# An int4 transformer layer: the down weights are dequantised inside the gate and up stage and pass through DRAM, with three direct pairs in place of five

## The reference

```python
w = stack([W_q >> 4 & 15, W_q & 15], axis=-1)          # per group of 64: (w - zero) * scale
g = x2 @ Wg.T ; u = x2 @ Wu.T                          # x2 = layernorm(x1), Wg and Wu: [2752, 1024]
h = silu(g) * u
out = x1 + layernorm(h @ Wd.T)                         # Wd: [1024, 2752]
```

## Time and profile before

| what | value |
|---|---|
| median of three runs | 2843.83 us |
| the profiled execution's own time | 2843.78 us |
| its span, first to last instruction | 2842.0 us |
| PE, DVE, ACT, POOL busy | 93%, 55%, 34%, 43% of the span |
| mean granted TensorE clock | 0.97 |
| time of a step in the 40 slices | 71 us |

### The profile page before, as it was taken

The page is one execution under the profiler, slowest core; times in us unless marked ns, Lnnn a source line. Parts: engine busy times, 40 slices in busy tenths (PEclk is TensorE's granted clock), DMA queues, the critical chain, the costliest instruction groups (busy, mean ns, idle before and its releaser), DMA issues. The chain is left out here.

```text
span 2842.0 us, 42348 instructions
## 1 busy us (share of the span) xinstructions
PE 2642.1 (93%) x17064; PEld 1116.6 (39%) x17064; DVE 1573.4 (55%) x1946; ACT 954.5 (34%) x1674; POOL 1220.0 (43%) x678
## 2 busy tenths in 40 slices
PE   6999899999999999989959989999999948499998
PEld 3445433333333333224424434444444413244443
DVE  6332777778778787525677686555555535300001
ACT  3111366666666666640112232222222211100000
POOL 0000277777777777742234434444444335300001
PEclk8999999999999999999979999999999979799999
DMA  4223101101011010022232122222222164323220
GB/s 168 76 78 91 29 17 31 42 16 29 20 40 29 16 29 1 1 82 97 103 88 62 52 55 75 75 74 75 74 75 75 37 195 134 113 85 123 69 69 30
DMA packets 200861, 187.16 MB, mean 66 GB/s; under 512 B 22512, under 2 KB 175600, under 8 KB 200688
## 3 DMA queue, kind: packets, MB, share of 16 engines
q1 hardware_dynamic: 188880, 177.02, 20.3%
q10 hardware_dynamic: 11808, 7.73, 1.0%
HBM read 134.74 MB, written 49.81 MB: 65 GB/s over the span
## 5 line engine op out<-in xcount | busy, mean ns | idle before, releaser
L728 POOL TENSOR_TENSOR c_prob<-c_prob 128x1024 f32<-128x1024 f32 (+1 forms) x288 | 605.1, 2120 | 517.8 <-ACT c_prob L626 515.2
L642 DVE TENSOR_REDUCE c_maxes<-c_s 128x2 f32<-128x1024 f32 (+3 forms) x640 | 645.7, 1058 | 196.1 <-PE c_s L482 196.1
L626 ACT ACTIVATE c_prob<-c_s 128x512 f32<-128x512 f32 (+1 forms) x1152 | 597.9, 571 | 299.3 <-PE c_s L504 185.3
L504 PE MATMUL c_s<-c_q,c_k 97*128 97x512 f16 (+3 forms) x1280 | 366.7, 352 | 10.1 <-ACT c_prob L626 1.7
L1182 PE MATMUL e_ps<-x_hi,e_w_hi 128*128 128x512 f16 x832 | 316.6, 381 | 16.1 <-DVE e_w_lo L1236 16.1
L1183 PE MATMUL e_ps<-x_lo,e_w_hi 128*128 128x512 f16 x832 | 316.6, 380 | 0.0
L1184 PE MATMUL e_ps<-x_hi,e_w_lo 128*128 128x512 f16 x832 | 316.4, 380 | 0.0
L1676 PE MATMUL f_yp<-f_wd_hi,f_h_hi 128*128 128x512 f16 x704 | 222.4, 383 | 84.5 <-DVE f_wd_lo L1738 76.9
L519 PE MATMUL c_ctx<-c_prob,v_sb 128*32 128x512 f32 (+3 forms) x2560 | 293.4, 539 | 0.2 <-ACT c_c L615 0.2
L1312 DVE TENSOR_TENSOR e_sums<-e_ps,e_sums 128x512 f32<-128x512 f32 x238 | 164.0, 689 | 229.3 <-PE e_ps L1184 227.7
L504 PEld LDWEIGHTS c_s<-c_q,c_k 97*128 97x128 f16 x1280 | 111.1, 97 | 345.2 <-ACT c_prob L626 298.7
(11 more groups left out here) (167 smaller groups left out, 3511.1 us busy)
## 6 DMA issues: line engine op xcount, KB each, us to landing
h_hi<-e_hh SPq DMA_DIRECT2D x84, 128.0 KB, 1.8
h_lo<-e_hl SPq DMA_DIRECT2D x84, 128.0 KB, 1.7
b_x<-L_attn_x SPq DMA_DIRECT2D x16, 512.0 KB, 6.1
c_q<-qk_hi SPq DMA_DIRECT2D x64, 128.0 KB, 3.1
d_x<-L_attn_x SPq DMA_DIRECT2D x16, 512.0 KB, 5.0
x_dram<-d_x SPq DMA_DIRECT2D x16, 512.0 KB, 2.6
out<-f_z SPq DMA_DIRECT2D x8, 1024.0 KB, 5.3
f_h_hi<-h_hi SPq DMA_DIRECT2D x6, 1344.0 KB, 8.5
```

Of the source, the lines that this page charges most:

```text
L504: last = nc.tensor.matmul(S2[:, h % 2, at:at + w], K[:, g % 2, k * P:(k + 1) * P], Q[:, g % 2, b, h, q:q + w], start=True, stop=not diag)
L626: nc.scalar.activation(prob(g, s, 0, w)[:, h, :], S2[:, h % 2, 0:w], ACT.Exp, scale=exp_scale).then_inc(exp_done, 1)
L642: last = nc.vector.tensor_reduce(MAXES[:, g % 2, t // TPB, heads, t % TPB, u], S1[:, heads, at:at + w], AX.X, ALU.max)
L728: return nc.gpsimd.tensor_tensor(one, one, two, ALU.add)
```

## The change

The pairs are now gate 0, rest, up 0 direct (`PLAIN = 3`), and 19 Strassen pairs. The T slices move into the first five units, two each in units (0,0), (0,1) and (2,0), one in (1,0) and (1,1); all eight tiles of T4 of the first half stand in unit (2,1), where the products run in another order. The 24 tasks of the down weights stand in gate_and_up, one in the first unit of each pair but pair 3, and two in each unit of the last pair; they are cut into `DH` and `DL`, and SP stores these into two DRAM tensors. Zeros and scales come in one DMA each per task, from tables that the host lays out in that order (the rest's task keeps its eighteen). The ring of `SUMS` is gone: a join writes into the tile of SILU or H where the next step works in place, and waits for that tile's last reader. project_down has no dequantisation; SP issues the loads of h and x, ScalarE's queue those of the weights, in six parts of growing size.

```diff
-    PLAIN = 5
-    pairs = [("gate", 0), ("up", 0), ("gate", 2), ("up", 2), ("rest", FULL)]
-    pairs += [(kind, c) for c in range(4, FULL - 1, 2) for kind in ("gate", "up")] + [("both", FULL - 1)]
+    PLAIN = 3
+    pairs = [("gate", 0), ("rest", FULL), ("up", 0)]
+    pairs += [(kind, c) for c in range(2, FULL - 1, 2) for kind in ("gate", "up")] + [("both", FULL - 1)]
...
+    downs = [(m, half) for m in range(FULL // 2 + 2) for half in range(2)]
+
+
+    tasks = [(0, i) + task for i, task in enumerate(tasks_of(0))]
+    AT_START = len(tasks)
+    beside, task_no, down_in = {}, {(0, i): i for i in range(AT_START)}, {}
+
+    def put(u, task):
+        beside.setdefault(u, []).append(len(tasks))
+        tasks.append(task)
+
+    for u in units:
+        q, p = u
+        if q + 1 < PAIRS and p < len(tasks_of(q + 1)):
+            task_no[q + 1, p] = len(tasks)
+            put(u, (q + 1, p) + tasks_of(q + 1)[p])
+        places = [1] if p == 0 and q + 1 < PAIRS and q != PLAIN else [0, 1] if q + 1 == PAIRS else []
+        for place in places:
+            number = sum(1 for t in tasks if t[2] == DOWN)
+            if number < len(downs):
+                down_in.setdefault(u, []).append(number)
+                put(u, (None, place, DOWN, number))
+    assert sum(1 for t in tasks if t[2] == DOWN) == len(downs)
...
+            return ["1", "2"]
+        if fast(q):
+            return ["P1", "P6", "P7", "P5", "P2", "P4", "P3"]
+        return ["12", "22", "11", "21"] if q == PLAIN - 1 else ["11", "12", "21", "22"]
...
+    made_beside = {(0, 0): [(0, 0), (0, 1)], (0, 1): [(0, 2), (0, 3)], (1, 0): [(1, 0)], (1, 1): [(1, 1)],
+                   (2, 0): [(1, 2), (1, 3)]}
     T_MADE = 3 * 2 * JC
-    REST_PAIR = PLAIN - 1
-    assert role(REST_PAIR) == "rest" and units[2 * JC] == (REST_PAIR, 0)
+    REST_PAIR = PLAIN - 2
+    assert role(REST_PAIR) == "rest"
...
-            return U2 if u + (name,) not in ring_of else SUMS[:, ring_of[u + (name,)], :], joined, join_no[u + (name,)]
+            return summed_in(u, name), joined, join_no[u + (name,)]
...
+                if kind == DOWN:
+                    words, scales, zeros = quantised[DOWN]
+                    half = downs[at][1]
+                    cols = slice(half * BANK, (half + 1) * BANK)
+                    for first, n, row in down_loads(at):
+                        g = row // RUN
+                        sp.dma_start(RAW[first:first + n, slot, :], words[row:row + n, cols]
+                                     ).then_inc(raw_loaded[slot], 16)
+                        for table, dst in ((zeros, ZEROS), (scales, SCALES)):
+                            sp.dma_start(dst[first:first + n, slot, :],
+                                         table[g:g + n // RUN, cols].unsqueeze(1).broadcast_to([n // RUN, RUN, BANK])
+                                         ).then_inc(raw_loaded[slot], 16)
...
+                elif kind is not None:
                     words, scales, zeros = quantised[kind]
-                    width = cols.stop - cols.start
-                    sp.dma_start(RAW[:, slot, :].rearrange("p (j i) -> p j i", j=JC)[:, :, into],
-                                 words.rearrange("(j p) i -> p j i", p=P)[:, :, cols]).then_inc(raw_loaded[slot], 16)
-                    for r in range(P // RUN):
-                        part = slice(r * RUN, (r + 1) * RUN)
-                        for table, dst in ((zeros, ZEROS), (scales, SCALES)):
-                            of_run = table.rearrange("(j r) i -> r j i", j=JC)[r:r + 1, :, cols]
-                            sp.dma_start(dst[part, slot, :].rearrange("p (j i) -> p j i", j=JC)[:, :, into],
-                                         of_run.broadcast_to([RUN, JC, width])).then_inc(raw_loaded[slot], 16)
+                    sp.dma_start(RAW[:, slot, :].rearrange("p (j i) -> p j i", j=JC),
+                                 words.rearrange("(j p) i -> p j i", p=P)[:, :, at * P:(at + 1) * P]
+                                 ).then_inc(raw_loaded[slot], 16)
+                    for table, dst in ((zeros, ZEROS), (scales, SCALES)):
+                        sp.dma_start(dst[:, slot, :], table[:, at * BANK:(at + 1) * BANK].unsqueeze(1)
+                                     .broadcast_to([P // RUN, RUN, BANK])).then_inc(raw_loaded[slot], 16)
...
+            def store_down(number):
+                m, half = downs[number]
+                n, planes = rows_of_words(tasks[down_task[number]])
+                c = 2 * m if planes == 2 else FULL - 1 + m - FULL // 2
+                cols = slice(half * BANK, (half + 1) * BANK)
+                for buf, done, dram, stored in ((DH, down_hi, wd_hi, down_hi_stored), (DL, down_lo, wd_lo, down_lo_stored)):
+                    sp.wait_ge(done, number + 1)
+                    sp.dma_start(dram[c * P:c * P + n * planes, cols].rearrange("(c p) d -> p c d", c=planes),
+                                 buf[0:n, 0:planes, :]).then_inc(stored, 16)
 
             for k in range(AT_START + 2):
                 load(k)
             for u in units:
-                if u in prepared and prepared[u] + 2 < len(tasks):
-                    load(prepared[u] + 2)
+                for k in beside.get(u, []):
+                    if k + 2 < len(tasks):
+                        load(k + 2)
+                for number in down_in.get(u, []):
+                    store_down(number)
...
+            def cut_down(number):
+                n, planes = rows_of_words(tasks[down_task[number]])
+                i = tasks[down_task[number]][1]
+                dve.wait_ge(down_hi, number + 1)
+                if number:
+                    dve.wait_ge(down_lo_stored, 16 * number)
+                nc.vector.scalar_tensor_tensor(DL[0:n, 0:planes, :], W[0:n, i, 0:planes, :], WS, DH[0:n, 0:planes, :],
+                                               ALU.mult, ALU.subtract).then_inc(down_lo, 1)
...
+                    out = summed_in(u, name)
+                    if key in silu_waits and silu_waits[key]:
+                        dve.wait_ge(h_done, silu_waits[key])
+                    if key in h_no and h_no[key] > 2:
+                        dve.wait_ge(lo_done, h_no[key] - 2)
...
                 if u in made_beside:
-                    of, j = made_beside[u]
-                    make_t1_t2(of, j)
-                    cut_t(of, 1, j)
-                    cut_t(of, 2, j)
-                    gated(u, names[0])
-                    cut_t(of, 3, j)
-                    for name in weight_cuts(q + 1)[:1] if p == 0 else weight_cuts(q + 1)[1:]:
+                    for n, (of, j) in enumerate(made_beside[u]):
+                        make_t1_t2(of, j)
+                        cut_t(of, 1, j)
+                        cut_t(of, 2, j)
+                        gated(u, names[n])
+                        cut_t(of, 3, j)
+                    for name in weight_cuts(q + 1)[p:p + 1]:
                         cut(q + 1, name)
-                    for name in names[1:]:
+                    for number in down_in.get(u, []):
...
+                    make_t4(0, 0)
+                    make_t4(0, 1)
                     gated(u, names[0])
-                    for j in (2 * p, 2 * p + 1):
-                        make_t4(0, j)
-                    cut(q + 1, weight_cuts(q + 1)[p])
+                    cut_t(0, 4, 0)
+                    cut_t(0, 4, 1)
+                    cut(q + 1, "S")
                     gated(u, names[1])
-                    for j in (2 * p, 2 * p + 1):
-                        cut_t(0, 4, j)
-                    for name in weight_cuts(q + 1)[2:] if p else []:
-                        cut(q + 1, name)
+                    make_t4(0, 2)
+                    make_t4(0, 3)
+                    gated(u, names[2])
+                    cut(q + 1, "W2")
+                    cut_t(0, 4, 2)
+                    cut_t(0, 4, 3)
+                    gated(u, names[3])
...
+
+
+    APART = 16
+    parts = [(0, 1), (1, 3), (3, 6), (6, 10), (10, APART), (APART, FULL)]
+    w_loaded, part_loaded = ([sem(f"f_{n}_loaded{i}") for i in range(len(parts))] for n in ("w", "part"))
...
-            for k in range(len(tasks)):
-                load_words(k)
+            for i, (first, end) in enumerate(parts):
+                for u in range(2):
+                    for buf, src in ((H_HI, h_hi), (H_LO, h_lo)):
+                        sp.dma_start(buf[:, u, first:end, :], src[first * P:end * P, rows(0, u)]
+                                     .rearrange("(c p) t -> p c t", p=P)).then_inc(part_loaded[i], 16)
+                        if end == FULL:
+                            sp.dma_start(buf[0:REST, u, FULL, :], src[FULL * P:, rows(0, u)]
+                                         ).then_inc(part_loaded[i], 16)
+            for u in range(2):
...
+                for c in range(APART):
+                    arrived(c)
                     for u in range(2):
                         for s in range(2):
```

(52 more changed lines are left out.)

315 lines of the change are left out of this document (139 added, 176 removed).

## The result

The changed kernel takes **2815.32 us** (median of 4 runs, 2810.35 to 2816.02); the kernel before, run beside it on the same chip, 2844.53. The ratio is 0.9895, 95% interval 0.9878 to 0.9912. The profiled execution took 2815.35 us, its span is 2813.6. So 29 us are gained where 61 were forecast, and the time lies 11 us above the range.

The account below looks back on a forecast made before the run. PE was taken to bound both changed stages. 2843.8 - 66.3 (project_down) + 2 (its load waits) + 3.6 (gate_and_up: -10.3 matmuls, -3.0 start, +16.9 head) = 2783 us; range 2764 to 2804.

Parts of the forecast that it names:

- The last stage: project_down's first round: PE starts after 6.5 us, not 33.9; 66.3 us back, less 2 us for waits on loads.
- rival B: project_down's first round: weights come late, about 18 us of waits, 2799 us in total; chance 0.10.
- D: Rival for units with a down task: VectorE's cut waits for late stores, +142 us, 2925 in total; chance 0.02.
- The first task's nine DMAs become three, 3.0 us: Start of gate_and_up: six issues at 0.48 us fewer, so PE starts 3.0 us earlier.
- The end, "nothing, or up to 2 us": End of gate_and_up: two down cuts of a unit wait for each other's stores, costing nothing or up to 2 us.
- A wait of VectorE for a down store: Sign in the profile of gate_and_up that would make the prediction wrong; no size given.
- The head, "waits 21.7, slow phases 7.5: 16.9 more": Head of gate_and_up: PE's waits 21.7 us against 9.8, slow phases 7.5 against 2.5, so 16.9 us more.
- VectorE's chain from PE's first matmul to W2 of pair 3: Head of gate_and_up: VectorE's listed slices, unpackings and cuts, from 1459.7 to 1600.5 us, 140.8 us.
- Rival C: Head of gate_and_up is worse: slices 10.9 us throughout, both T4 pairs 11; 7 + 5.5 us more, 2796; chance 0.13.
- the unpackings and cuts: VectorE's operations in the head of gate_and_up: 2.0 us per task's unpacking, 1.1 us per weight cut.

Follow-up runs that it names:

- e6: The kernel before, with only the change's single four-row load per table for gate and up tasks (three per task, not nine): 2844.77 us, ratio 1.0006.
- e1: The changed kernel with each table row written four times in DRAM, so a load reads 16 rows for 8 partitions each: 2796.30 us, ratio 0.9841.
- e2: The changed kernel with each table loaded by four DMAs of 32 partitions, as in the kernel before: 2801.49 us, ratio 0.9854.
- e4: The edits of e3 and e1 together on the changed kernel: 2773.43 us, ratio 0.9759.
- e5: e1 without the down tasks beside pairs 0 to 2; the last three tasks are not computed, extra stores fill their place: 2793.24 us, ratio 0.9825.
- e8: The kernel of e1 run once more without an edit: 2794.03 us, one run.
- e3: The changed kernel with five direct pairs instead of three and one T slice in each of eight units, tables unchanged: 2788.97 us, ratio 0.9811.
- e7: The changed kernel run once more without an edit: 2815.79 us, one run.

## Why the prediction was right and wrong

1. **The last stage was right.** Forecast: PE after 6.5 us, no wait, 66.3 - 2 = 64.3 us back. Measured: 7.8 us, and 554.1 - 488.3 = 65.8 back. That the sum is so close is luck in part: PE's start gave 26.1 for 27.4, what follows 39.7 for 36.9. The loads keep up: no wait in the round; rival B, late weights, did not come (the windows 2330 to 2360 us show 381 and 388 GB/s, above both rates that I had). Nor did D: the steady part is at 100%.
2. **"The first task's nine DMAs become three, 3.0 us" is the first step that failed, in its sign.** I counted issues at 0.48 us and took the landing as unchanged (1.7 us). The three landed after 7.2. Measured +5.2 in place of -3.0: 8.2 us. e6 shows it without the change's other parts, e1 and e2 undo it. The step fails in its size as well: with three transfers of 16 rows (e1) the start takes 13.2 us, so 0.3 of the 3.0 us come.
3. **The end, "nothing, or up to 2 us", was right in kind and wrong in size: 6.5.** I named the place, two down cuts in a unit that wait for each other's stores, and priced a store as landing promptly. Behind four-row tables it took 9.6 us; in e1 it took 4.0, and the end was back at 6.6. A wait of VectorE for a down store was also named as a sign that the prediction is wrong, and this is one.
4. **The head, "waits 21.7, slow phases 7.5: 16.9 more", was the right mechanism at half its size, and this is the largest error.** Measured: waits 38.5 for 9.8, 28.7 more; with 10.3 us less of matmuls and a stretch 23.5 us longer, 23.5 + 10.3 - 28.7 = 5.1 for slow phases, as taken. So 33.8 in place of 16.9. VectorE's chain from PE's first matmul to W2 of pair 3 took 153.3 us in place of 140.8. Reading it slice by slice gives the terms of these 12.5. In unit (0,0) the load of the down task kept it waiting 1.5 us longer, the two slices took 20.8 for 20.0, and each of the two cuts 2.1 where I had 1.1: 1.9. Where two unpackings stand in one unit, the second meets GpSimd's scaling of the first: 2.3 us in (1,0), 3.3 in (2,0); in (1,1) the one unpacking meets GpSimd's lo cut of a tile of H, 1.0. And a slice with its gated tile took 12.7 for 11.6, twice; the two of unit (2,0) 23.8 for 21.4. Against that (0,1) was 2.9 shorter. Of the other 4.4 us, 2.7 are the two waits in unit (5,0), where PE was forecast at 100%; 1.7 were not taken apart. The rows of one such meeting, timeline of unit (2,0):

```profile
1565.82 3.56 DVE L1313 TENSOR_SCALAR e_nibbles<-e_raw 128x512 int32<-128x512 int32 x1
1566.76 2.34 POOL L1622 TENSOR_TENSOR e_w<-e_w,e_scales 128x1024 f32<-128x1024 f32 x1
```

The row of 0.42 us of the earlier trace rows takes 3.56 here: it spans GpSimd's operation in whole and ends 0.3 us after it. I had charged such waits to sums of slices alone and costed each unpacking at 2.0. By the rule of the Trainium skill, SBUF — State Buffer, section "SBUF: two separate sides", an operation of VectorE with one input can be shut out as well when it runs in one of its fast modes; the row agrees with a lock, and whether this operation ran in such a mode no run here shows. Rival C had this direction and 12.5 of the 16.9 us, but by other terms: of its long slices only part came (0.8 and 2.4 us).
5. **Not priced at all: 2.2 us before the stage.** The code there is untouched (last section).

The differences sum: 8.2 + 6.5 + 16.9 + 2.2 - 1.5 = 32.3, and 2815.3 - 2783 = 32.3. The step that failed most is the head's term: the forecast took the unpackings and cuts in a chain of 140 us on a full engine at their shortest rows, 2.0 and 1.1 us. The chain was 12.5 us longer, PE's waits to its end 14.1, and the range had room for such an error alone, not with the loads' 8.2 and the end's 6.5 beside it.

## What to carry to other kernels

Fewer transfers are not cheaper transfers: look at the rows that one has in DRAM, and at the busy share of the queues while they are all that runs (0.38 against 0.76 here for the same bytes). With a good shape three transfers and nine differed by 0.3 us at the start. Where an engine has no idle time over many units, price its chain from the longest rows with each neighbour on the shared side, and count every operation that moves into the stretch, for each microsecond there is the bound engine's. Two changes that share a diff can be of opposite sign: storing the down weights gave 65.8 us, while the two further Strassen pairs, with down tasks beside them, cost a net 24.8.

## What the runs showed that was not expected

The stages before gate_and_up are the same code in all these kernels, yet the first gate load comes at 1446.5 to 1446.7 us in e1, e4, e5 and e8, at 1449.2 in the kernel before, at 1450.0 in e6, and at 1451.4 to 1452.0 in the changed kernel, e2, e3 and e7. Of the 4.8 us between the changed kernel and e1, 0.5 arise by 65 us, 2.8 at the start of `attend` and 1.5 at 324 to 328 us (granted clock 0.97 in the window 300 to 350 us against 1.00). Timelines of PE and windows 255 to 265 us, first of the changed kernel run once more (e7), then of e8:

```profile
256.93 0.37 PE L548 MATMUL c_s<-wv_hi,c_hi 128*128 128x256 f16 x1 [3.79 <-PEq L121]
```

```profile
255.00:260.00 5.00, 3.08 (x15) 2.23 (x16) 2.20 (x1) 0.00 (x0) 0.00 (x0) 0.59 0.52 167
260.00:265.00 5.00, 5.00 (x36) 3.93 (x35) 1.27 (x1) 0.38 (x1) 0.00 (x0) 0.72 0.75 194
```

```profile
256.25 0.27 PE L548 MATMUL c_s<-wv_hi,c_hi 128*128 128x256 f16 x1 [3.79 <-PEq L121]
```

```profile
255.00:260.00 5.00, 3.75 (x35) 3.39 (x36) 2.87 (x1) 0.38 (x1) 0.00 (x0) 1.00 0.57 189
260.00:265.00 5.00, 5.00 (x49) 4.49 (x47) 0.60 (x1) 0.77 (x2) 0.00 (x0) 1.00 0.72 200
```

The same idle time of 3.79 us is followed by matmuls at 0.59 and 0.72 in the one, mostly at the 1.2 GHz level (0.37 us for the first), and by full clock in the other (0.27 us); 51 matmuls in these ten microseconds against 84. The first profiles of the two kernels have the same (0.57 and 0.75; 1.00 and 1.00), so in two profiles of each it went with the program. What decides it stays open: the spread kernels differ there in nothing but the size of tables that are read much later. Whether every execution of a kernel does the same isn't shown either: one of the four runs of the changed kernel took 2810.35 us, 5 less than the others, and the unprofiled runs of e1 took 2.1 to 4.2 us more than the profiled one.

So 4.8 of the 21.2 us between the profiled spans of the changed kernel and e1, and 5.2 of the 7.5 between e2 and e1, are not the loads' doing. A forecast of a change in one stage of this kernel can be off by 5 us for a reason in another.
